# A transformer block on one core: the written-out order of five engines, their stage distances and the PSUM banks laid out anew

## The reference, cut to what matters

```
xn  = layernorm(x);  q, k, v = xn, ctx, ctx in 16 heads of 16
qf  = exp(q*s @ F) + 1e-4                       # 64 random features a head
kf  = exp(k*s @ F + h_k - max over ALL batches of h_k) + 1e-4
num, den = causal sums over tokens of qf.kf*v and qf.kf
x1  = x + tanh(g_xattn) * num/den
y   = layernorm(x1);  h = rmsnorm(y)*gamma1
q   = h@Wq + bq;  k, v = (h@Wdown + bdown)@Wup + bup
att = softmax over the 16 heads g of (q_h . k_g / 4)   # per token, heads attend heads
y2  = y + (att v)@Wo + bo
h2  = rmsnorm(y2)*gamma2;  gate = softmax(h2@Wg + bg)  # 8 experts
out = x1 + tanh(g_ffn) * (y2 + sum_e gate_e * h2@We_e)
```

## Time and profile before

| | |
|---|---|
| three runs | 1117.64, 1119.69, 1121.66 us; median 1119.69 |
| the profiled execution | 1119.66 us; its span, first to last instruction, 1117.9 us |
| busy, of the span | PE 1034.7 us (93%), weight loads 841.2 (75%), DVE 938.5 (84%), ACT 757.0 (68%), POOL 756.8 (68%) |
| PE instructions | 12867 matmuls |
| transfers | 38.63 MB, mean 35 GB/s, nearly all in the first 40 us |
| mean granted clock of TensorE | 0.991 |

### The profile page before, as it was taken

How to read it: one execution, slowest core, us unless ns; L and a number is a source line. 1 busy time by engine, 2 the same in 40 slices (tenths; PEclk the granted TensorE clock), 3 DMA queues, 4 the chain that set the end, 5 groups by cost and what they waited for, 6 DMA issues and landing times.

```text
span 1117.9 us, 31579 instructions
## 1 busy us (share of the span) xinstructions
PE 1034.7 (93%) x12867; PEld 841.2 (75%) x12867; DVE 938.5 (84%) x2173; ACT 757.0 (68%) x1563; POOL 756.8 (68%) x1111
## 2 busy tenths in 40 slices
PE   0576899999999999999999999999999999999988
PEld 0355677778888888778888787888778888888776
DVE  7578678888888988888888888888888988888886
ACT  6666767667776776777677667776776677767531
POOL 3467776677767767777777667776767777777431
PEclk9988899999999999999999999999999999999999
DMA  9410000100001001010010101000000000000000
GB/s 307 142 29 11 21 30 1 30 30 30 30 30 29 11 21 30 30 30 30 30 31 2 29 30 30 30 30 30 24 8 31 29 31 30 30 30 12 11 11 19
DMA packets 38911, 38.63 MB, mean 35 GB/s; under 512 B 3440, under 2 KB 38512, under 8 KB 38768
## 3 DMA queue, kind: packets, MB, share of 16 engines
q1 hardware_dynamic: 38384, 36.59, 10.5%
q0 software_dynamic: 384, 0.04, 0.0%
HBM read 28.23 MB, written 8.39 MB: 33 GB/s over the span
## 4 chain that ended last, share of the span: by engine, by line
PE 52%; DVE 24%; DMA 7%; ACT 7%; POOL 6%; issue 2%; SPq 1%; POOLq 0%; DVEq 0%; ACTq 0%
PE ps L1857 10%; PE ps L1858 7%; PE ps L1859 7%; DVE z L1142 6%; PE ps L1888 6%; PE ps L1903 5%; PE ps L1872 4%; DMA c_in<-in_ctx 4%; DMA x_in<-in_x 3%; PE ps L1937 3%; PE ps L1896 3%; POOL x L424 2%; POOL z L417 2%; DVE k_t L1426 2%; PE ps L1851 2%
## 5 line engine op out<-in xcount | busy, mean ns | idle before, releaser
L1142 DVE SCALAR_TENSOR_TENSOR z<-ps,gate,z 128x256 f32<-128x256 f32 x512 | 234.5, 470 | 17.4 <-PE ps L1859 8.9
L1857 PE MATMUL ps<-we_hi,h_hi 128*128 128x512 f32 (+2 forms) x640 | 238.8, 373 | 5.8 <-DVE s_sub L1296 1.7
L1858 PE MATMUL ps<-we_lo,h_hi 128*128 128x512 f32 (+2 forms) x640 | 223.7, 350 | 0.0
L1859 PE MATMUL ps<-we_hi,h_lo 128*128 128x512 f32 (+2 forms) x640 | 223.7, 349 | 0.0
L1857 PEld LDWEIGHTS ps<-we_hi,h_hi 128*128 128x128 f32 x640 | 120.2, 188 | 44.3 <-issue 18.5
L1888 PE MATMUL ps<-qf,kf 64*128 64x256 f32 x1024 | 137.4, 397 | 11.7 <-POOL qf L408 9.4
L1859 PEld LDWEIGHTS ps<-we_hi,h_lo 128*128 128x128 f32 x640 | 120.2, 188 | 17.2
L1858 PEld LDWEIGHTS ps<-we_lo,h_hi 128*128 128x128 f32 x640 | 120.5, 188 | 11.6
L1888 PEld LDWEIGHTS ps<-qf,kf 64*128 64x128 f32 x1024 | 95.1, 191 | 36.9 <-issue 19.1
L1903 PE MATMUL ps<-att,v 128*32 128x256 f32 (+1 forms) x2048 | 112.4, 339 | 1.2 <-DVE att L1218 0.9
L475 POOL TENSOR_SCALAR v_bd<-v_t,sel_blk 128x512 f32<-128x512 f32 x128 | 88.3, 710 | 13.2 <-DVE v_t L1249 13.2
(11 more groups left out here) (218 smaller groups left out, 3077.9 us busy)
## 6 DMA issues: line engine op xcount, KB each, us to landing
x_in<-in_x SPq DMA_DIRECT2D x32, 256.0 KB, 3.3
c_in<-in_ctx SPq DMA_DIRECT2D x32, 256.0 KB, 3.7
out<-z SPq DMA_DIRECT2D x32, 256.0 KB, 2.2
c_chunk<-in_ctx SPq DMA_DIRECT2D x14, 512.0 KB, 8.9
stage<-in_L_ffn_We SPq DMA_DIRECT2D x2, 1024.0 KB, 9.6
c_chunk<-in_ctx SPq DMA_DIRECT2D x2, 256.0 KB, 8.5
stage_u<-in_L_ffn_Wup SPq DMA_DIRECT2D x2, 128.0 KB, 5.7
stage_b<-in_L_ffn_bup SPq DMA_DIRECT2D x1, 256.0 KB, 6.1
```

Of the source, the lines that this page charges most:

```text
L1142: return dve.scalar_tensor_tensor(out=z[b % 2][:, t, :], in0=ps[:, bank, offset:offset + D], scalar=gate[:, t, ex:ex + 1], in1=z[b % 2][:, ...
L1857: pe.matmul(out, a_hi(c), b_hi(c), start=(c == 0), stop=False)
L1858: pe.matmul(out, a_hi(c), b_lo(c), start=False, stop=False)
L1859: last = pe.matmul(out, a_lo(c), b_hi(c), start=False, stop=(c == C - 1))
```

## The change

```diff
-BANK = dict(stab=0, fk0=2, fk1=7, fk2=1, fk3=4, fq0=1, fq1=0, fq2=7, fq3=2, x000=6, x001=1, x010=7, x011=5,
-            y00=4, y01=3, av0=2, x100=6, x101=0, x110=4, x111=7, y10=2, y11=3, av1=3, nd0=5, nd1=6, ht=3,
-            dn=0, qq=7, kv0=4, kv1=3, s=5, pv0=0, pv1=1, otr=5, o=0, h20=4, h21=7, mm0g=5, mm1g=6, mm00=1,
-            mm01=0, mm02=7, mm03=2, mm10=4, mm11=7, mm12=2, mm13=5)
+BANK = dict(stab=0, fk0=6, fk1=4, fk2=3, fk3=7, fq0=0, fq1=2, fq2=4, fq3=1, x000=3, x001=1, x010=0, x011=5,
+            y00=3, y01=7, av0=3, x100=0, x101=2, x110=5, x111=4, y10=1, y11=6, av1=2, nd0=2, nd1=0, ht=1,
+            dn=7, qq=1, kv0=7, kv1=5, s=7, pv0=0, pv1=1, otr=4, o=1, h20=3, h21=6, mm0g=3, mm1g=6, mm00=5,
+            mm01=3, mm02=5, mm03=5, mm10=4, mm11=6, mm12=2, mm13=5)
...
             def fkp_(b):
-                if b >= 2:
-                    pe.wait_ge(*at("bqq", b - 2))
-                pe.wait_ge(*at("k_lo", b))
...
+                if b >= 0:
+                    pe.wait_ge(*at("k_lo", b))
...
+                if b >= 3:
+                    pe.wait_ge(*at("ssub", b - 3))
+                if b:
+                    pe.wait_ge(*at("x111", b - 1))
+                if b >= 1:
+                    pe.wait_ge(*at("y11", b - 1))
                 feature_products("k", k_hi, k_lo, more=True)
...
+            load_bqkv_()
+            load_wdn_()
+            load_wq_()
+            load_c_(2)
+            load_wg_()
             load_x_(1)
-            load_wdn_()
-            load_wg_()
-            load_bqkv_()
-            load_wo_()
-            load_wq_()
-            load_we_()
+            load_we_()
+            load_wo_()
```

More of the change, by code:

```diff
@@ L192, in build @@
             signal("once_pe0", "most_turned stab_all"),
[L193 to L198, removed]
+            signal("pe0", "fk fq X00 X01 Y0 X11"),
+            signal("pe1", "X10 av3 nt_t"),
@@ L199, in build @@
+            signal("pe2", "av0 av1"),
+            signal("pe3", "hn_t qq s"),
+            signal("pe4", "dn kv0"),
+            signal("pe5", "kv1 pv"),
+            signal("pe6", "o_tr o"),
+            signal("pe7", "h2_t1 mm1g mm10 mm11"),
+            signal("pe8", "h2_t0 mm0g mm00 mm01"),
+            signal("pe9", "mm12 mm13"),
+            signal("pe10", "mm02 mm03"),
+            signal("once_dve0", "zero_f zero_v1 v1_one least_ least stabilizer less0 less"),
             signal("keys_dve0", "key_sums"),
@@ L209, in build @@
-            signal("dve9", "a0g"),
+            signal("dve1", "c_t"),
+            signal("dve2", "q_st q_mv q_bn x_t"),
+            signal("dve3", "y00 y01 y10 den_s den_d den o_x"),
+            signal("dve4", "y11 g_st g_mv g_bn"),
+            signal("dve5", "ht_lo bqq q_t v_t smax ssub"),
+            signal("dve6", "d_lo bkv0 k_t p_t"),
+            signal("dve7", "bkv1 o_tok s_rec"),
+            signal("dve8", "ot_lo y2"),
+            signal("dve9", "h2_lo1 ga gmax gm gsum grec gate a1g a10_ a10 a11_ a11"),
@@ L217, in build @@
[L217 to L227, removed]
+            signal("act1", "k_hi ek2"),
@@ new lines, in build @@
+            signal("act2", "h_t"),
+            signal("act3", "xn q_hi eq0"),
+            signal("act4", "ek0 x000 x010 x100"),
+            signal("act5", "ek3 eq2 x001 x011 x110"),
+            signal("act6", "ek1 eq1 nt0"),
+            signal("act7", "eq3 x101 nt1"),
+            signal("act8", "x111"),
+            signal("act9", "hn ht_hi d_hi q_bd"),
+            signal("act10", "k_bd p_bd ot_hi"),
+            signal("act11", "y"),
+            signal("act12", "sq h2n h2_hi1"),
+            signal("act13", "h2_hi0 gexp"),
@@ new lines, in o_ @@
+            @per_batch
+            def o_(b):
+                if not b:
+                    pe.wait_ge(*at("bqq", b + 1))
+                if b >= 2 and b + 3 < NB:
+                    pe.wait_ge(*at("eq3", b + 3))
+                pe.wait_ge(*at("ot_lo", b))
+                for t in range(T):
+                    last = three_passes(ps[:, BANK["o"], t * D:(t + 1) * D], tok(ot_hi, t), tok(ot_lo, t), cols(wo_hi, 0, D), cols(wo_lo, 0, D))
+                last.then_inc(*up("o", b))
+            @per_batch
@@ new lines, in Y1_, with X11_ @@
+            @per_batch
+            def Y1_(b):
+                if b >= 4:
+                    pe.wait_ge(*at("a11", b - 4))
+                pe.wait_ge(*at("x001", b))
+                second_keys(b, 1, BANK["y10"], BANK["y11"])
+            @per_batch
+            def X11_(b):
+                if b == 4:
+                    pe.wait_ge(*at("a00", b - 4))
+                pe.wait_ge(*at("x011", b))
+                first_keys(b, 1, 1, BANK["x110"], BANK["x111"]).then_inc(*up("X11", b))
+            @per_batch
@@ new lines, in X10_, with av0_ @@
+            def X10_(b):
+                if b >= 4:
+                    pe.wait_ge(*at("a12", b - 4))
+                if b == 2:
+                    pe.wait_ge(*at("x010", b))
+                first_keys(b, 1, 0, BANK["x100"], BANK["x101"]).then_inc(*up("X10", b))
+            @per_batch
+            def av0_(b):
+                pe.wait_ge(*at("m00", b))
+                if b == 4:
+                    pe.wait_ge(*at("v1", b))
+                pe.wait_ge(*at("y00", b))
+                attend(0, 0, BANK["av0"]).then_inc(*up("av0", b))
@@ new lines, in s_, with av1_ @@
+            @per_batch
+            def s_(b):
+                pe.wait_ge(*at("k_bd", b))
+                if b >= 0:
+                    pe.wait_ge(*at("q_bd", b))
+                if b + 2 < NB:
+                    pe.wait_ge(*at("y01", b + 2))
+                head_scores(BANK["s"]).then_inc(*up("s", b))
+            @per_batch
+            def av1_(b):
+                if b >= 0:
+                    pe.wait_ge(*at("m01", b))
+                if b >= 0:
+                    pe.wait_ge(*at("y01", b))
+                attend(0, 1, BANK["av0"]).then_inc(*up("av1", b))
```

2779 lines of the change are left out of this document (1698 added, 1081 removed).

## The result

| | median, us | runs | ratio to before, 95% interval |
|---|---|---|---|
| before | 1120.68 | 1117.64 to 1123.62 (4) | |
| after | 1077.24 | 1076.46 to 1077.5 (4) | 0.9611 (0.9584 to 0.9639) |
| after, a second time | 1077.25 | 1075.18 to 1078.1 (5) | 0.9621 (0.9589 to 0.9653) |

The change makes the kernel 3.8% faster, some 43 us. The forecast was 1087 with 1068 to 1108: the sign, and over the steady slots the size, came out; the head gained about twice what was put down for it.

The account below looks back on a forecast made before the run. The prediction took PE (TensorE) to bound the kernel, with DVE next. Steady slots -21, head -8 and end -4 sum to -33 us, span 1117.9 to 1084.9, forecast 1087 us with range 1068 to 1108.

Parts of the forecast that it names:

- PE bounds, and the slot would be 31.28: Steady slots: PE sets the pace; a slot falls from 32.12 to 31.28 us, saving 21 us over 25 slots.
- Two excursions less, two changes of kind more: -0.35: PE's steady order: fewer tiled stretches between full matmuls, -0.60 us a slot; more switches of tile kind inside them, +0.25.
- New waits 0.25 for old ones of 0.74: PE in steady slots: the old waits of 0.74 us a slot go, and new small ones of 0.25 come.
- The POOL chain: Steady slot, end of o to av0: 8.0 us of DVE and POOL work plus handoffs against PE's 8.2, no slack.
- The ACT chain to `mm00`: Steady slot, end of X01 to mm00: about 6.4 us of pieces less overlaps against PE's 5.9, no slack.
- `q_bn`'s wait for `x_in` put down as nothing: Steady slots: this wait, 21.6 us over 18 slots before, was given no cost since DVE isn't the bound.
- the 0.40 that come and go: Steady slots of before: PE waits making the mean slot 0.40 us longer than the shortest, 31.72; fkp on bqq shows.
- Head -8: First nine slots: a quarter of PE's idle time and work lost to the clock is saved, -8 us (+5 to -18).
- End -4: Last five slots: more work beside batch 31's chain saves half of 7.8 us idle, -4 us (0 to -6).
- `x_in(1)` behind the weights, taken as 0: Head: this load, now behind 1.15 MB of other loads, could come late by up to 4 us; taken as 0.
- Everything fits: Rival for the whole kernel: slots of 30.9 us, head -16, end -5, giving 1069 us; chance 0.12.
- The POOL chain sets the slot: Rival for steady slots: v_bd ahead of the masks delays av0 and what follows, +23 us, giving 1142; chance 0.08.

Follow-up runs that it names:

- e3: Kernel after, with PE's expert product mm03 moved ahead of fk, so PE enters the tiled steps four times a slot, not three: 1083.13 us, ratio 0.9692 to before.
- e5: Kernel before, with PE's expert product mm1g moved one slot earlier, directly ahead of fkp, four tiled stretches a slot instead of five: 1127.89 us, ratio 1.0095 to before.
- e6: Kernel before, with a third buffer for x_in and its load issued one slot earlier: 1112.2 us, ratio 0.9949 to before.
- e1: Kernel after, with the steady loop starting at slot 3 instead of 6 on all queues, replacing the lists of slots 3 to 5: 1078.8 us, ratio 0.9651 to before.
- e2: Kernel after, with the lists of the last five slots replaced by the steady loop on all five queues: 1101.92 us, ratio 0.9856 to before.
- e4: Kernel after, with POOL's v_bd and k_lo moved behind the masks m01, m00 and g_r: 1121.43 us, ratio 1.0037 to before.
- e8: Kernel after, with POOL's v_bd moved behind the two masks m01 and m00 alone: 1106.8 us, ratio 0.9901 to before.

## Why the forecast was right, and where it was not

- *PE bounds, and the slot would be 31.28.* It is 31.28. The saving over the slots came out at -20.4 (24 of them) for -21 (25).
- *Two excursions less, two changes of kind more: -0.35.* e3 measures one of each at 0.17, so -0.34 for two. That the sum came out is in part luck, since both prices in it were too low and the two errors nearly cancel. `fq` of before, between `mm10` and `kv1`, is an excursion by itself (PE's timeline):

```profile
596.34 0.40 PE L1859 MATMUL ps<-we_hi,h_lo 128*128 128x512 f32 x1
596.67 0.50 PE L1872 MATMUL ps<-q_hi,f_hi 32*128 32x512 f32 x4
597.01 0.40 PE L1872 MATMUL ps<-q_hi,f_lo 32*128 32x512 f32 x4
597.24 0.40 PE L1872 MATMUL ps<-q_lo,f_hi 32*128 32x512 f32 x4
597.57 0.39 PE L1921 MATMUL ps<-wup_hi,down 128*128 128x256 f32 x1
597.80 0.28 PE L1922 MATMUL ps<-wup_lo,down 128*128 128x256 f32 x1
```

The distances are 0.33, 0.34, 0.23, 0.33 and 0.23; without a change they would be four times 0.23 and, for 256 columns, 0.12. So an excursion costs four times some 0.10, not three: the forecast left out that the first tiled matmuls are held too. It had that share in its own numbers, as the 0.11 in `X11`. A change of kind costs the 0.20 that it read at `av1` and `X11`, where it took 0.15: `av3` ahead of `fk` takes 0.76 (626.88 to 627.64) for the 0.67 of `av0` ahead of `s`, and `fk` 0.11 more. Either way one border between kinds costs about 0.20, 0.10 on each side. Before has 11 of them in a slot, after 9, which gives -0.40; e3 adds one, and e5 takes one away for 0.20. (Into steps on 32 columns only the share ahead of it shows; both kernels have two of these in a slot.)

- *New waits 0.25 for old ones of 0.74.* By the difference, 0.84 less 0.35 to 0.40 leaves 0.44 to 0.49 for the waits, near 0.74 - 0.25. The POOL chain was called in the right place (`av0` for `m00`), and it misses by 0.13. The ACT chain to `mm00` shows no wait on PE; what holds PE for ACT is `Y0` behind `x000`, by about 0.10, which the forecast hadn't named and no run takes away.
- *`q_bn`'s wait for `x_in` put down as nothing.* Too little was said there: the wait is gone in after, and e6 shows that it alone was worth 0.22 us a slot. The total came out because these waits were already counted at PE's end, as the 0.40 that come and go. The step that was weak is "DVE isn't the bound, so I put nothing down for it".
- *Head -8.* This is the failed term: -18.6, or -15.7 with the postponed 2.9 us. Between 39.6 us and batch 7's first keys PE idles 19.5 us of 196.2, where before it idled 28.2 of 214.8, and at a mean clock of 0.97 for 0.95, which is worth about 5 (0.05 x 214.8 less 0.03 x 196.2). "A quarter of idle and lost work" had no row behind it. e1 shows why it was too little: the new order fills DVE, ACT and POOL to 90 us and more of the 116 from the first batches on, and the steady time is reached in slot 4. Slot 80.2 to 106.6, which was read for it, had no engine busy for over 84% of it: there chains, not engines, set the time. That the change shortened these chains is what the fuller engines suggest; no run takes one of them apart.
- *The clock.* It was granted 0.91 from 39.6 to 155.5 us before and 0.96 after: some 21 us of the stretch at 1.2 GHz before and some 10 after. PE has 9 pauses of over 1 us there before and 6 after. By the Trainium skill, TensorE: Matmul & The Clock Gate (HAM oscillation), which the forecast weighed, the cost of coming back to full clock is paid again after each pause that throttles the array; the trace agrees, and the case that it was raised for, that the head could keep none of its gain, did not come.
- *End -4.* -3.3, and -6.2 as work. Right in size, but the reason is e2's: not more work beside batch 31's chain, but a list that saves some 24 us, of which the new order would lose 20 against before in draining.
- *`x_in(1)` behind the weights, taken as 0.* `bn_stats` of batch 1 runs at 36.6 us with no wait, and batch 0's first keys come at 45.07 for 44.77. Right.
- *Rivals.* "Everything fits" (1069) was nearer in time than the forecast, but by the head, not by its slots of 30.9. "The POOL chain sets the slot" did not come with the change, and came at once when POOL's order was touched (e4: 1121, e8: 1107).

What stays open: how the head's gain divides between the new order and the lists of slots 0 to 2, and why two small operations of DVE sometimes take 1.25 us longer.

## What to carry to other kernels

Where an engine is 99% busy, time the start-to-start distances of its steps: what is to be had lies in boundaries between kinds of work and in waits too short to look like idle time, here 0.84 us of 32. In such an order steps can't be moved one by one: an excursion saved (e5) or a mask put first (e4, e8) meets an input that isn't ready, and an in-order queue passes that wait to everything behind it, so look first at what the moved step was covering. An order tuned for the middle must have its end checked by itself, since the steps that run out first are those that gave the others time.

## What was not expected of the hardware

- Four operations of POOL, 2.9 us together, moved behind two of 0.65 us cost 1.24 us in every slot on an engine that is 74% busy (e8): the share of idle time alone says nothing about slack in its order.
- Around a pause of PE of 4.75 us the granted clock is 0.89 over 31 us (e2, 1044 to 1075), where after has 1.00.
- Two operations of DVE on two columns take 0.35 and 0.68 us in most slots and 0.94 and 1.33 in some, and end within 0.02 us of a POOL operation either way. PE's `s` comes 1.25 us later for it, in none to three of the steady slots of a profiled execution (e1, e2, e3).
- A change between matmuls on the full array and on parts of it costs about 0.10 us ahead of it and 0.10 behind it, at 1.00 of the clock, and PE shows as busy throughout.
